# A decoder layer on one core: the copy that clears the sorted rows is issued later in the program

## The reference, cut to what matters

```python
x = _layernorm(x + attention(x, Wkv, bkv, Wq, bq, Wp, bp))            # (8, 512, 256), 16 heads of 64
x = _layernorm(x + cross_attention(x, ctx_1024, cos, sin, ...))       # context (8, 1024, 256)
x = _layernorm(x + experts(x, Wr, rb, W1, W2, W3, Ws1, Ws2, Ws3))     # 8 experts, 2 of them per token
```

```python
kv = inputs @ Wkv + bkv;  k, v = jnp.split(kv, 2, axis=-1);  q = inputs @ Wq + bq
attn = softmax(einsum('sbhd,tbhd->bhst', q, k) * SCALE)
out  = einsum('bhst,tbhd->sbhd', attn, v).reshape(s, b, H * HD) @ Wp + bp
```

## Time and profile before

| | |
|---|---|
| median of 3 runs | 3116.47 us |
| the profiled execution | 3117.52 us, of it a span of 3115.8 us |
| PE busy | 2872.5 us (92% of the span) |
| DVE, ACT, POOL busy | 2203.1, 1436.4, 1583.5 us |
| queue of ACT's DMA (q10) | 10,000 packets, 10.38 MB, 1.4% of 16 engines' span |
| queue of SP's DMAs (q1) | 120,992 packets, 149.51 MB, 15.7% |

### The profile page before, as it was taken

One profiled execution on the slowest core, in us unless ns is written; L12 is line 12 of the kernel. 1 busy time (PEld: TensorE's weight loads), 2 busy tenths in 40 slices (PEclk: granted clock), 3 DMA queues, 4 the chain that ended last, 5 costly groups with the idle time before them and its releaser, 6 DMA issues. The chain is left out here.

```text
span 3115.8 us, 52151 instructions
## 1 busy us (share of the span) xinstructions
PE 2872.5 (92%) x17256; PEld 1967.6 (63%) x17256; DVE 2203.1 (71%) x3447; ACT 1436.4 (46%) x2079; POOL 1583.5 (51%) x1053
## 2 busy tenths in 40 slices
PE   5999999969999999999999999999999969899996
PEld 4888888854553553554554554454455449899995
DVE  3555555567788788678778778777777873588886
ACT  2222222245455554554554554654554632455554
POOL 1222222227447547547546546645645616477875
PEclk9999999989999999999999999999999989999998
DMA  9000000020010010010010010010010024477876
GB/s 264 15 15 15 15 15 16 15 61 14 11 40 14 11 42 11 11 42 11 15 41 9 14 42 8 14 42 8 14 42 8 14 85 156 144 201 217 234 217 180
DMA packets 145591, 182.42 MB, mean 59 GB/s; under 512 B 17040, under 2 KB 107408, under 8 KB 145296
## 3 DMA queue, kind: packets, MB, share of 16 engines
q1 hardware_dynamic: 120992, 149.51, 15.7%
q0 software_dynamic: 14304, 18.75, 3.6%
q10 hardware_dynamic: 10000, 10.38, 1.4%
HBM read 115.92 MB, written 45.90 MB: 52 GB/s over the span
## 5 line engine op out<-in xcount | busy, mean ns | idle before, releaser
L825 POOL TENSOR_SCALAR raw<-raw 128x1024 f32<-128x1024 f32 x416 | 684.0, 1644 | 191.9 <-ACT raw L1080 171.8
L1080 ACT ACTIVATE raw<-b_ps 128x1024 f32<-128x1024 f32 x416 | 410.7, 1021 | 365.2 <-PE b_ps L854 317.2
L967 PE MATMUL b_ps<-raw 128*64 128x512 f32 x1664 | 422.3, 610 | 57.2 <-POOL raw L825 57.2
L1231 DVE TENSOR_TENSOR b_acc<-b_acc,raw 128x1024 f32<-128x1024 f32 x304 | 399.2, 1313 | 89.9 <-POOL raw L825 80.3
L811 POOL TENSOR_TENSOR b_knat<-raw,b_knat 128x512 fp32r<-128x512 f32 x128 | 165.2, 1291 | 402.5 <-ACT b_knat L1034 402.5
L846 PE MATMUL b_ps<-b_QH,b_KT 128*128 128x512 f32 x1024 | 324.1, 429 | 14.4 <-ACT raw L1080 8.8
L846 PEld LDWEIGHTS b_ps<-b_QH,b_KT 128*128 128x128 f32 x1024 | 168.3, 189 | 244.3 <-issue 157.2
L1691 PE MATMUL c_ps<-c_xT_l,c_w_h 128*128 128x256 f32 x1504 | 308.6, 288 | 6.7 <-DVEq L1933 3.5
L967 PEld LDWEIGHTS b_ps<-raw 128*64 128x64 f32 x1664 | 95.5, 136 | 277.4 <-POOL raw L825 160.8
L1691 PEld LDWEIGHTS c_ps<-c_xT_l,c_w_h 128*128 128x128 f32 x1504 | 245.4, 193 | 13.3 <-DVEq L1933 6.0
L1204 DVE RECIPROCAL b_r<-b_ps 128x128 f32<-128x128 f32 x256 | 239.1, 944 | 16.5 <-PE b_ps L874 15.0
(11 more groups left out here) (262 smaller groups left out, 7093.9 us busy)
## 6 DMA issues: line engine op xcount, KB each, us to landing
c_raw<-in_L_ffn_W_dram SPq DMA_DIRECT2D x117, 512.0 KB, 6.1
b_QH<-b_QH SPq DMA_DIRECT2D x128, 128.0 KB, 2.4
xs<-zeros ACTq DMA_DIRECT2D x1, 10140.0 KB, 67.3
c_xg<-xs SPq DMA_DIRECT2D x39, 260.0 KB, 7.2
b_rows<-in_ctx_dram SPq DMA_DIRECT2D x9, 1024.0 KB, 6.2
a_xt<-in_x_dram SPq DMA_DIRECT2D x72, 64.0 KB, 2.1
b_rows<-x SPq DMA_DIRECT2D x9, 512.0 KB, 5.6
x<-a_x1t SPq DMA_DIRECT2D x64, 64.0 KB, 1.9
```

What stands on the lines that cost most here:

```text
L825: pool.tensor_scalar(pr, pr, HI, LO, ALU.min, ALU.max).then_inc(clipped, 1)
L967: mm = pe.matmul(bank(key)[hh * HD:(hh + 1) * HD, :], V[:, t, (2 * p + hh) * HD:(2 * p + hh + 1) * HD], place(unit(p, j, a))[:, hh * B:(hh ...
L1080: ins = act.activation(place(unit(p, j, a)), both(key), ACT.Exp, scale=SCALE)
L1231: dve.tensor_tensor(total, total, pr, ALU.add).then_inc(acc_ready, 1)
```

## The change

The DMA itself stays as it is; it is written into a function `clear` that ACT calls inside stage a, after the high parts of all four weights and after the wait for the constants, and ahead of its loop over chunks. The opening block keeps its POOL part and has no ACT part any more.

```diff
@@ self_attention, ACT
                 for n in range(1, 4):
                     weights.split_hi(act, n)
                 act.wait_ge(consts_in, 64)
+                clear(act)
                 with act.Fori(0, CH) as c:
@@ build
-            @block.scalar
-            def _(act):
+            def clear(act):
+
                 act.wait_ge(made, 5)
                 act.dma_start(xs.rearrange("(p t) d -> p t d", p=P), zeros[:, :].unsqueeze(1).broadcast_to([P, ROUTED // P, ROW])
                               ).then_inc(xs_clear, 16)
```

More of the change, by code:

```diff
@@ L108, in three_terms, with self_attention @@
     return ((w_hi, x_hi), (w_hi, x_lo), (w_lo, x_hi))
-def self_attention(nc, x, Wkv, bkv, Wq, bq, Wp, bp, x1_dram, ident, identb, raw, loaded, load_next):
+def self_attention(nc, x, Wkv, bkv, Wq, bq, Wp, bp, x1_dram, ident, identb, raw, loaded, load_next, clear):
     CH, TT, BI = 8, 4, 16
@@ L2027, in _ @@
                 pool.memset(zeros[:, :], 0.0).then_inc(made, 1)
-            @block.scalar
-            def _(act):
-                act.wait_ge(made, 5)
-                act.dma_start(xs.rearrange("(p t) d -> p t d", p=P), zeros[:, :].unsqueeze(1).broadcast_to([P, ROUTED // P, ROW])
-                              ).then_inc(xs_clear, 16)
         x2_dram = x2_out if x2_out is not None else nc.dram_tensor("x2", (S, B, D), F32, kind="Internal").ap()
@@ L2039, in build @@
             loaded = [[attention.enter_context(nc.semaphore(f"{name}_w_loaded{n}")) for n in range(4)] for name in "ab"]
+            def clear(act):
+                act.wait_ge(made, 5)
+                act.dma_start(xs.rearrange("(p t) d -> p t d", p=P), zeros[:, :].unsqueeze(1).broadcast_to([P, ROUTED // P, ROW])
+                              ).then_inc(xs_clear, 16)
             def load_next(sp):
@@ L2045, in build @@
             if "a" in upto:
-                self_attention(nc, x, aWkv, abkv, aWq, abq, aWp, abp, x1_dram, ident, identb, raw, loaded[0], load_next)
+                self_attention(nc, x, aWkv, abkv, aWq, abq, aWp, abp, x1_dram, ident, identb, raw, loaded[0], load_next,
+                               clear)
             else:
```

## The result

The changed kernel's median over 9 runs was 3088.45 us (3078.57 to 3098.91), beside 3114.64 us for 9 runs of the kernel before. The ratio of the two is 0.9935 with a 95% interval of 0.9912 to 0.9958: 0.65% less, or 20 us of 3115, with an interval of 13 to 27 us. The forecast was 3098, so 18.2 us won.

A forecast was written before the change was run, and what follows sets the result against it. The opening's weight loads, slowed by the clear beside them, were taken to bound the first Q tile's matmul; moving it from 50.01 to 31.8 wins 18.2 us, 3117.52 to 3099.3, or 3098 at the median. Range 3091 to 3109.

The forecast's parts named there:

- What bounds: Opening: PE waits on a chain of casts whose idle times each end with a load on SP's queue, slowed by the clear.
- hand-over: Start of the first Q tile's matmul, 50.01 us before; from there PE works without a gap that a load ends.
- The barrier: End of the opening block: ends with POOL's zeros at 2.39 instead of ACT's issue at 3.00; worth 0.6 us.
- K's weights and x: First loads of the opening: K's weights there at 8.5 us, x at 10.2, so PE starts 9.2 us earlier.
- From x to Wp: SP's queue behind x: small bias pieces 4 us, bv and bp 2.1; V's weights land at 19.7, Q's 23.1, Wp 26.5.
- 4-byte pieces: 2048 pieces of the bq and bk loads on SP's queue, taken as 4 us, with ends of nothing and 12.4 us.
- The chain behind: From DVE's low part of V's weights at 21.7, 10.1 us to the first Q tile at 31.8; by Wp 31.5.
- The sum: First Q tile from 50.01 to 31.8: 18.2 us won, 3099.3 for an execution like the profiled one, 3098.3 at the median.
- The new place: Clear issued by ACT at 28.5 behind the casts, landing near 96; ACT not held, 20 us cover for x; price 0.
- Loads slow by themselves: Rival, opening: K's weights and x stay late without the clear; 9.6 us won, 3107, or 3115; chance 0.08.
- The second chunk of x: Rival, PE's second transposes: PE waits for x if its block takes over 20 us longer; up to 3116; chance 0.02.
- ACT was not held: Answers the slower rival: ACT held at the clear's issue, first Q copy at 95.8, 44 us slower, 3160; chance 0.03.

## Why the prediction was right

*What bounds.* Right: the hand-over moved, and nothing behind it gave anything back.

*The barrier.* 0.6 us forecast, 0.98 measured (SP's first issue at 2.69, not 3.67).

*K's weights and x.* Forecast 8.5 and 10.2, measured 9.21 and 11.63. Right in size, but the reason was half of one: the prediction spoke of a clear that runs beside the loads. What held K's weights was that the clear had been issued first. The kernel with both issued together has K's cast at 9.34 with the clear running. From SP's first issue, K's weights took 6.5 us where 5.4 had been counted, and x 8.9 where 7.1 had been; the barrier's extra 0.4 us hid part of that.

*From x to Wp.* The 4-byte pieces were counted at 4 us; they cost 2.5. The rate of 0.30 MB per us was low for the 4 KB pieces of V's and Q's weights: Q's cast started 2.6 us behind V's (18.47, 21.09), where 3.4 had been counted. V's cast was forecast at 19.7 and came at 18.47, Wp's at 26.5 and came at 23.90.

*The chain behind.* The 10.1 us from V's low part to the hand-over were 10.04 (30.54 - 20.50). PE's slow pace after its idle time was rightly left out of the sum here: before tile 4 PE waited 0.4 us, and tile 4's first matmul took 0.51 us. That it can cost something is seen in three other profiles, where PE had been idle for 1.86 to 2.79 us ahead of the hand-over and lost 1.5 us behind it.

*The sum.* 18.2 forecast, 19.5 measured in the profiles and 19.5 and 20 in the runs. The 1.3 us too little come from V's weights, which were 1.2 us early. That this miss is so small is partly luck: x came 1.4 us late, and from x to V's weights it took 6.8 us where 9.5 had been counted, so a term too short and terms too long nearly cancelled. The late x itself cost nothing, because DVE was still behind: PE had 0.4 us to spare at tile 4. The median of the runs after, 3088.45, lies 9.6 us under 3098. The runs of either kernel spread over 20 us and more, and the median of the kernel before was 3116.47 in the first three runs and 3100.38 in 23 later ones; so the forecast is to be held against the ratio.

By the experiments the 19.5 us are made up so: 6.1 from the head start and the barrier (50.01 to 43.94), 9.8 from the clear beside x, the small pieces and the order of issue ahead of V's weights (to 34.13), 3.6 from the clear beside V's, Q's and Wp's (to 30.54). Read at the second transposes, where PE's slow pace behind the hand-over counts as well, the same three are 6.1, 8.3 and 5.1 us (100.69, 94.61, 86.31, 81.21).

*The new place.* Right: ACT was not held (0.59 us), the clear was issued 4.5 us sooner than forecast, and PE did not wait for x. The clear took 55.3 us to land where 67.3 had been counted. The kernel with the clear at the end of stage a has no shorter way from the hand-over to the second transposes (50.7 us in both), so its price behind the casts is nothing.

*The rivals.* "Loads slow by themselves" fell with K's cast at 9.21. The second chunk of x was no matter: PE did not wait for it. ACT was not held: its first Q copy came 1.7 us behind the first Q matmul, as before.

## What to carry to other kernels

A large copy that nobody awaits soon belongs behind the last load that somebody awaits, in time and not only on another queue; here the same 10 MB cost 19.5 us in the opening, some 19 us at the next stage's start, and nothing behind the casts. Look at the packets per queue in the first microseconds: if the queue that matters moves none, the other had a head start. And compare stretches between fixed instructions, not spans, where two profiles of one kernel differ by 9 us in a loop.

## What the runs showed of the hardware that was not expected

- A queue issued 1.3 us ahead of the other kept the 16 DMA engines until 5.6 us after the other's first issue (1360 packets against 1); issued together, both moved from the start (408 and 261); with SP's queue ahead, it was the clear that stood back (521 and 103). A head start of 0.8 us for a third of the clear gave the same picture (1351 against 8). The equal counts from 20 to 30 us agree with turns. The first 6 us after a head start do not: 1360 pieces are 85 for each of 16 engines, against one.
- The same 2048 pieces of 4 bytes cost V's weights 2.5 us without the clear and 9.5 us beside its 1040-byte pieces.
- Pieces of 520 bytes went at nearly the same number per us as pieces of 1040 bytes (229 and 206), so the clear in half pieces took 100.7 us to land instead of 67.3.
- 80 more matmuls on PE, ahead of everything, made an untouched loop 4 us longer per turn, half by waits and half by a lower granted clock; the cause stays open.
